# Softmax denominators of four heads in one group of matmuls, reciprocals spread by small transfers

## The reference

```python
xn  = layernorm(x)                       # x: 8 x 512 x 128, float32
qkv = xn @ W_qkv + b_qkv                 # 16 heads of 64
A   = softmax(q @ k.T / 8) per head      # 512 x 512
att = (A @ v) @ W_out + b_out
for t in range(8):                       # a gated recurrence over the 8 batches, from in_c
    c = sigmoid(xn[t] @ wf.T + c @ uf.T + bf) * c + sigmoid(xn[t] @ wi.T + c @ ui.T + bi) * tanh(xn[t] @ wc.T + c @ uc.T + bc)
out = x + att + tanh(xn @ wo.T + c @ uo.T + bo)
```

## Time and profile before

| | |
|---|---|
| median of the runs | 944.82 us |
| the profiled execution | 947.0 us |
| its span, first to last instruction | 945.2 us |
| mean granted TensorE clock | 0.976 of full |
| PEld busy | 570.3 us, 60% |
| DVE busy | 571.0 us, 60% |
| ACT busy | 447.0 us, 47% |

### The profile page before, as it was taken

How to read it: one execution, slowest core, us unless ns; L and a number is a source line. 1 busy time by engine, 2 the same in 40 slices (tenths; PEclk the granted TensorE clock), 3 DMA queues, 4 the chain that set the end, 5 groups by cost and what they waited for, 6 DMA issues and landing times.

```text
span 945.2 us, 14913 instructions
## 1 busy us (share of the span) xinstructions
PE 889.6 (94%) x5429; PEld 570.3 (60%) x5429; DVE 571.0 (60%) x770; ACT 447.0 (47%) x579; POOL 547.4 (58%) x270
## 2 busy tenths in 40 slices
PE   4769899899999999999999999999999999999988
PEld 3445666665666666665666666665666566666553
DVE  6756465564666646664666556665666476664632
ACT  4325545444555534552555554552455455553441
POOL 4033543545777746774677666773677577773664
PEclk9679999999999999999999999999999999999999
DMA  7000000000000000000000000000000000000000
GB/s 223 1 0 1 1 24 1 1 12 2 24 12 2 11 0 34 0 11 0 34 0 11 0 0 34 0 11 0 34 0 11 0 22 11 0 12 1 12 12 11
DMA packets 18635, 13.75 MB, mean 15 GB/s; under 512 B 1298, under 2 KB 16176, under 8 KB 18608
## 3 DMA queue, kind: packets, MB, share of 16 engines
q1 hardware_dynamic: 18608, 13.39, 4.6%
HBM read 6.83 MB, written 2.10 MB: 9 GB/s over the span
## 4 chain that ended last, share of the span: by engine, by line
PE 87%; DVE 9%; ACT 2%; issue 1%; DMA 0%; SPq 0%; DVEq 0%
PE st L744 19%; PE pv L758 13%; PE misc L758 12%; PE mx L725 8%; PE st L690 7%; DVE NM L508 6%; PE mx L774 6%; PE mx L768 6%; PE st L750 5%; PE misc L690 3%; PE misc L647 3%; PE pv L647 2%; PE mx L647 2%; PE pv L690 1%; ACT probs L360 1%; DVE AT L462 1%
## 5 line engine op out<-in xcount | busy, mean ns | idle before, releaser
L508 DVE TENSOR_REDUCE NM<-mx 128x2 f32<-128x1024 f32 x256 | 313.9, 1226 | 174.4 <-PE mx L725 174.2
L360 ACT ACTIVATE probs<-st 128x1024 f32<-128x1024 f32 x256 | 258.3, 1027 | 107.8 <-PE st L750 97.2
L251 POOL TENSOR_TENSOR AT<-AT,RD 128x512 f32<-128x512 f32 x63 | 80.7, 1280 | 256.0 <-DVE RD L526 196.6
L259 POOL TENSOR_TENSOR PSUMK<-probs 128x1024 f32<-128x1024 f32 x64 | 153.1, 2393 | 109.2 <-ACT probs L360 109.2
L265 POOL TENSOR_TENSOR PSUMK<-PSUMK,probs 128x1024 f32<-128x1024 f32 x64 | 152.8, 2387 | 8.2 <-ACT probs L360 2.7
L272 POOL TENSOR_TENSOR PSUMK<-PSUMK,probs 128x1024 f32<-128x1024 f32 x64 | 152.5, 2383 | 6.1
L758 PE MATMUL misc<-probs,VALL 128*64 128x512 f32 x512 | 130.2, 592 | 0.0
L725 PE MATMUL mx<-KH,QH 64*128 64x512 f32 x512 | 114.7, 442 | 13.7 <-DVE NM L508 11.5
L758 PE MATMUL pv<-probs,VALL 128*64 128x512 f32 x512 | 124.7, 606 | 0.0
L744 PE MATMUL st<-QH,KH 64*128 64x512 f32 x512 | 109.0, 420 | 0.8 <-ACT probs L360 0.6
L522 DVE STREAM_TRANSPOSE RD<-mx 128x512 f32<-128x512 f32 x63 | 45.1, 716 | 103.3 <-PE mx L768 103.3
(11 more groups left out here) (179 smaller groups left out, 1237.4 us busy)
## 6 DMA issues: line engine op xcount, KB each, us to landing
probs<-in_L_attn_data_dram SPq DMA_DIRECT2D x4, 512.0 KB, 7.4
XSH<-XH SPq DMA_DIRECT2D x8, 256.0 KB, 2.4
XSL<-XL SPq DMA_DIRECT2D x8, 256.0 KB, 2.4
RES<-in_L_attn_data_dram SPq DMA_DIRECT2D x8, 256.0 KB, 2.7
out_dram<-RES SPq DMA_DIRECT2D x8, 256.0 KB, 2.3
probs<-in_L_attn_W_qkv_dram SPq DMA_DIRECT2D x3, 512.0 KB, 4.5
MROW<-TM SPq DMA_DIRECT2D x64, 4.0 KB
WO<-in_L_attn_W_out_dram SPq DMA_DIRECT2D x1, 512.0 KB, 4.5
```

Of the source, the lines that this page charges most:

```text
L259: nc.gpsimd.tensor_tensor(PSUMK[:, s % 2, :, :], e[:, :, 0, :], e[:, :, 1, :], ALU.add).then_inc(sum_part, 1)
L360: nc.scalar.activation(probs[:, s % 2, :, u, :], st[:, u % 2, :, :], ACT.Exp, scale=SCALE).then_inc(exp_done, 1)
L508: nc.vector.tensor_reduce(NM[:, 0:4 * TB].rearrange("p (h a b) -> p h a b", h=2, a=2)[:, :, s % 2, b], mx[:, :, :], AX.X, ALU.max, negate= ...
```

## The change

- `sums` is called once per stretch, for both pairs, behind all values (in the last stretch ahead of the second pair's values). It has four matmuls of 32 columns, one per head, whose results stand in the four quarters of one bank, `st[:, 1, 1]`. The matmuls of scores that write this bank next wait for DVE (`den_used`).
- DVE makes one transpose and one set of reciprocals per stretch, for four heads (`divisors`). The reciprocals of a head then stand on 32 partitions; eight transfers of SP (`spread_divisors`, 32 partitions by 16 numbers each) put them on the head's 64 partitions in a new tile `RX`, for two pairs. Two transposes fill `RD` from `RX` (`fill_divisors`); they stand between the second and the third reduction of the next stretch, behind a wait for the transfers.
- POOL's two `normalise` move behind the first three sums of the next stretch; the last pair but one is normalised at the very end.

```diff
+            def spread_divisors(n, j):
+
+                sp.wait_ge(r16_done, STRETCHES * n + j + 1)
+                sp.sem_inc(passed_sp, 1)
+                for a in range(2):
+                    for h in range(2):
+                        for m in range(2):
+                            sp.dma_start(RX[HD * h + 32 * m:HD * h + 32 * m + 32, a, :],
+                                         R16[32 * (2 * a + h):32 * (2 * a + h) + 32, :]).then_inc(d_r, 16)
...
                     if j == 3 and not first:
                         sp.wait_ge(out_rows, 16 * n)
                         sp.sem_inc(passed_sp, 1)
+                    spread_divisors(n, j)
...
-                wait(pool, den_done, t - 1)
+                wait(pool, den_done, STRETCHES * n + j)
...
-                    if not (first and j == 0):
-                        normalise(t - 1, s - 1)
                     for k in range(2):
-                        first_sum(t + k, s + k)
+                        first_sum(n, j, t + k, s + k)
                         second_sum(t + k, s + k)
                         third_sum(t + k, s + k)
-                    normalise(t, s)
+                        if k == 0 and not (first and j == 0):
+                            normalise(t - 2, s - 2)
+                            normalise(t - 1, s - 1)
 
             batches(pool, step)
+            normalise(8 * N - 2, PAIRS - 2)
...
-            def divisors(t, s, source):
-
-                r = RD[:, s % 2, :]
-                dve.wait_ge(den_done, t + 1)
-                wait(dve, norm_done, t - 1)
-                nc.vector.transpose(r, source).then_inc(den_used, 1)
-                dve.wait_ge(den_used, t + 1)
-                nc.vector.reciprocal(R16[:, :], r.rearrange("p (c j) -> p c j", j=32)[:, :, 0]).then_inc(r16_done, 1)
-                dve.wait_ge(r16_done, t + 1)
-                nc.vector.transpose(r.rearrange("p (c j) -> p c j", j=32),
-                                    R16[:, :].unsqueeze(2).to_broadcast([P, L // 32, 32])).then_inc(rd_done, 1)
+            def divisors(n, j):
+
+                dve.wait_ge(den_done, STRETCHES * n + j + 1)
+                wait(dve, norm_done, 8 * n + 2 * j)
+                nc.vector.transpose(RD[:, 0, :], st[:, 1, 1, :]).then_inc(den_used, 1)
+                dve.wait_ge(den_used, STRETCHES * n + j + 1)
+                wait(dve, d_r, 128 * (STRETCHES * n + j))
+                nc.vector.reciprocal(R16[:, :], RD[:, 0, :].rearrange("p (c j) -> p c j", j=32)[:, :, 0]).then_inc(r16_done, 1)
+
+            def fill_divisors(n, j):
+
+                dve.wait_ge(d_r, 128 * (STRETCHES * n + j + 1))
+                for a in range(2):
+                    nc.vector.transpose(RD[:, a, :].rearrange("p (c j) -> p c j", j=32),
+                                        RX[:, a, :].unsqueeze(2).to_broadcast([P, L // 32, 32])).then_inc(rd_done, 1)
...
                         maxima(t + 2, s + 2, 0, STRETCHES * n + j + 1)
-                        for b in range(1, TB):
-                            maxima(t + 2, s + 2, b)
+                        maxima(t + 2, s + 2, 1)
+                    if not (first and j == 0):
+                        fill_divisors(n, j - 1)
+                    if coming:
+                        maxima(t + 2, s + 2, 2)
+                        maxima(t + 2, s + 2, 3)
...
-                    divisors(t, s, mx[:, 1, :])
-                    divisors(t + 1, s + 1, mx[:, 0, :] if coming else st[:, 0, 0, :])
+                    divisors(n, j)
 
             batches(dve, step)
+            fill_divisors(N - 1, 3)
...
-            def sums(t, s, dst):
-
-                pe.wait_ge(sum_done, t + 1)
-                for h in range(2):
-                    last = nc.tensor.matmul(dst[OWN[h], :], ones[:, :], PSUMK[:, s % 2, h, :], start=True, stop=True)
+            def sums(t):
+
+                pe.wait_ge(sum_done, t + 2)
+                for a in range(2):
+                    for h in range(2):
+                        g = 32 * (2 * a + h)
+                        last = nc.tensor.matmul(st[g:g + 32, 1, 1, :], ones[:, 0:32], PSUMK[:, a, h, :], start=True,
+                                                stop=True, tile_position=(0, g))
                 last.then_inc(den_done, 1)
...
                         pe.wait_ge(tm_done, STRETCHES * n + j + 1)
-                        wait(pe, den_used, t)
+                        if first:
+                            wait(pe, t_done, 3 * s - 1)
+                        elif j == 1:
+                            pe.wait_ge(o_evac, n)
+                        elif j == 2:
+                            pe.wait_ge(out_done, n)
                         score_maxima(t + 2, s + 2, 0)
                         pe.wait_ge(q_lo, t + 4)
                         pe.wait_ge(k_lo, t + 4)
                     scores(n, t, s, 0)
+                    wait(pe, den_used, STRETCHES * n + j)
                     scores(n, t, s, 1)
...
-                    if first:
-                        pe.wait_ge(t_done, 3 * s + 5)
-                    elif j == 0:
-                        pe.wait_ge(o_evac, n)
-                    elif j == 1:
-                        pe.wait_ge(out_done, n)
-                    sums(t, s, mx[:, 1, :])
...
-                    if coming:
-                        values(n, t + 1, s + 1, (0, 1))
-                        pe.wait_ge(tm_done, STRETCHES * n + j + 2)
-                        sums(t + 1, s + 1, mx[:, 0, :])
-                        values(n, t + 1, s + 1, (2, 3))
-                    else:
-                        sums(t + 1, s + 1, st[:, 0, 0, :])
-                        values(n, t + 1, s + 1)
+                    if not coming:
+                        sums(t)
+                    values(n, t + 1, s + 1)
+                    if coming:
+                        if ahead:
+                            pe.wait_ge(k_lo, t + 6)
+                        sums(t)
```

More of the change, by code:

```diff
@@ L66, in build_block @@
         R16 = sb("R16", [P, L // 32])
+        RX = sb("RX", [P, 2, L // 32])
         RD = sb("RD", [P, 2, L])
@@ L142, in build_block @@
         sum_part, sum_done, norm_done, last_norm = sem("sum_part"), sem("sum_done"), sem("norm_done"), sem("last_norm")
-        d_m = sem("d_m")
+        d_m, d_r = sem("d_m"), sem("d_r")
         d_xs, d_res, out_rows = sem("d_xs"), sem("d_res"), sem("out_rows")
@@ L252, in normalise, with first_sum @@
                                         ALU.mult).then_inc(norm_done, 1)
-            def first_sum(t, s):
+            def first_sum(n, j, t, s):
                 pool.wait_ge(exp_done, 4 * t + 2)
-                wait(pool, den_done, t - 1)
+                wait(pool, den_done, STRETCHES * n + j)
                 e = probs[:, s % 2, :, :, :]
```

## The result

The changed kernel took 1095.3 us (median of 4 runs, 1095.1 to 1098.9) beside 944.9 for the kernel before (4 runs, 944.7 to 945.3): ratio 1.160, 95% interval 1.158 to 1.162. Forecast: 1079, in a range of 1020 to 1110.

What follows compares the result with a forecast made beforehand. TensorE's order was taken to bound every stretch. +4.56 us at 27 starts (+123), +4.2 in the first batch, +2.8 and +4.5 at the end: +135 on 947.0, less 2.2, gives 1079 us; range 1020 to 1110.

Steps and rivals of the forecast that it cites:

- The three parts of the table: Forecast loss by place: 4.2 us up to batch 1, 118.6 over 26 stretches, 11.9 from there to the end.
- What bounds it: Whole kernel: TensorE, busy 94%, sets each stretch's length; a term costs what it adds to its order or waits.
- The sums: Sums on TensorE: one group replaces two, saving 0.86 us per stretch, less 0.25 for the change of shape.
- four tiles do not overlap: Sums on TensorE: the four matmuls run two at a time, so the saving is absent; 1106 us, chance 0.10.
- VectorE at the boundary: VectorE behind the sums: transpose and reciprocal delay the second matmul group of maxima by 0.29 us.
- The transfers: Ahead of the third reduction: eight issues 0.60 us apart delay the filling, and TensorE stands 3.92 us per stretch.
- the rival built on that rule: VectorE's wait before the filling: all transfers land before the second reduction ends; 943 us (938 to 950), chance 0.04.
- The clock: TensorE around the stall: the clock falls to half speed, costing 1.2 us per stretch, bounds 0 and 3.0.
- more at half speed: TensorE behind the stall: low clock costs 1.8 us more at 27 starts; 1127 us, heavier cases together chance 0.11.
- the clock holds: TensorE behind the stall: no fall of clock, 27 x 1.2 us less; 1047 us, chance 0.13 for 1022 to 1047.
- First batch: First batch: sums save 0.61 us four times; three stalls swallow a 2.01 us hole, no clock added; +4.2 us.
- The last stretch: Kernel's end: output projection waits for POOL's later normalisation, +2.8 us, and the final filling comes later, +4.5 us.

Runs made afterwards that it cites:

- the first experiment: Changed kernel with the filling transposes behind the next stretch's reductions, POOL's normalisations one sum group later than planned and the projection in two parts: 947.0 us, ratio 1.001.
- the fifth experiment: the first experiment with the one reciprocal moved behind the first reduction, leaving VectorE only the transpose ahead of it: 938.9 us, ratio 0.9926.
- second experiment: Changed kernel with the filling transposes in place but reading R16 without waiting for the transfers, so divisors go to wrong heads: 950.4 us, ratio 1.0045.
- third: Changed kernel with four of the eight transfers, half of the division left out: 973.8 us, ratio 1.029.
- the fourth experiment: Changed kernel with 22 extra unused matmuls on TensorE in the stall, in every stretch behind the first: 1048.7 us, ratio 1.108.

## Why the prediction was right, and where it was off

The sign, the place and the mechanism came as forecast; the time came 16 us above 1079, inside the range. The three parts of the table miss by 4.4, 4.8 and 4.2 us; the rest is mostly the 2.2 us that the forecast took off for the profiled execution, which this time was no slower than the median. By its own steps:

*What bounds it.* Right: a stretch is TensorE's order, and a stall in front of M3 went into the time in full. With the wait moved out of TensorE's way (the first experiment), no stall in front of M3 is left and 148 of the 150 us are gone.

*The sums.* Right in sign, a little cautious: M0 runs at S+0.99 where I had 1.11. Four matmuls of 32 columns do run side by side, eight records and the change to the next shape in 0.99: the first four start within 0.02 us of each other, the next four 0.45 behind them. The rival "four tiles do not overlap" is out by that row. The Trainium skill's 2.38 times for three such tiles (*TensorE: Matmul & The Clock Gate*, Part 3), by which the group alone would have taken an estimated 1.08, isn't seen here: group and change of shape together took 0.99. How the 0.99 divides between the group and the change behind it was not measured apart; in all the merge is worth 0.68 per stretch, where my terms gave 0.61.

*VectorE at the boundary.* r0 was forecast for S+2.28 and came at 2.53 in the stretch shown (0.40 "issue" in front of it, a batch's start), and earlier in the others. M1 is 0.11 late in three stretches of four and 0.65 in the fourth, where I had 0.29 for all: 0.25 as the mean. That this is the price of the reciprocal in front of r0 is shown by the fifth experiment.

*The transfers.* Right, and by the term that I was least sure of. First issue at S+2.23 (forecast 2.44), distance 0.625 (0.60), all in at S+8.37 (8.44), and r2 at 9.60 (9.87): the two filling transposes take 1.23 to the next instruction and not 1.42. M3 stands 4.01 later than before relative to M0 (9.85 for 5.84), forecast 4.21. Of this 3.3 is the wait and 0.5 to 0.7 VectorE's transposes (second experiment), and each transfer costs 0.635 (third). *DMA: Bandwidth & Descriptors* of the Trainium skill (Issuing engines are not separate DMA queues) has it that initiating a DMA is usually small beside the DMA; here a 2 KB transfer holds SyncE for 0.625 us and lands 1.7 after its issue began, eight take 5.00 us to issue, and the rival built on that rule (938 to 950) is refuted.

*The clock.* The largest miss of a term, and in the direction of the "more at half speed" rival. I had 1.2 us per stretch, with one episode of 3.4 us of which 1.1 would lie in the stall. Three of the 26 stretches had no low clock, and were 3.15 to 3.19 longer than before; 17 had 3.4 us of it, and six had 6.8. From 123.4 in all and 3.17 for the stall and its neighbours, 1.57 is left per stretch: 41 us for the 26, where I had 31 (2.3 of the 41 are the late transfers of three stretches). The two kinds differ in price and in where the fall came:

```profile
291.60:298.40 6.80, 5.84 (x28) 4.62 (x30) 3.29 (x3) 2.05 (x2) 4.87 (x4) 0.50 0.01 2
568.10:571.50 3.40, 3.40 (x18) 2.66 (x16) 1.21 (x1) 1.16 (x2) 2.88 (x3) 0.50 0.00 0
```

In the 17 stretches the fall came between 0.5 us ahead of M3 and 1.5 behind it (M3 is at 567.54 in the second row's stretch), so nearly the whole episode lay on work, and it cost 1.3 to 1.5 us. In the six it came 0.6 to 1.3 ahead of M3 (M3 is at 292.56 in the first row's), the clock stayed down twice as long, and it cost 2.3 to 2.6. I had the fall 1.1 ahead with one episode; that combination occurs in none of the 26. Reading the first batch as "each time" was also too strong: the same four waits of 1.85 us stand in the first experiment, and two of them were followed by a low clock. The stall, on the other side, was a little cheaper than my terms (3.17 for 3.36 without the clock), so that in the sum of the 26 stretches two misses, +10 and -5, partly cancel. The rival "the clock holds" (1047) is close to what the fourth experiment measured once TensorE was kept busy, 1048.7.

*First batch.* The step that was most wrong for its size: +8.6 for +4.2. I let the stall swallow the hole of 2.01 behind M3 and counted no clock, "its clock falls already". The hole did shrink (M3 to the next matmul is 0.73 instead of 2.25, 1.5 us back), but the first twelve of the gate projection's eighteen records behind it ran at half clock, 0.43 apart, as in these rows of the kernel after:

```profile
145.66 0.80 PE L746 MATMUL mx<-KH,QH 64*128 64x512 f32 x2 [3.66 <-DVE NM L521]
146.39 0.80 PE L668 MATMUL pv<-XH,gwH 128*128 128x512 f32 x1
146.98 0.63 PE L668 MATMUL pv<-XH,gwL 128*128 128x512 f32 x1
```

Two of the batch's four stretches had 6.8 us at half clock instead of 3.4. It is 0.8 us in this stretch (6.75 us from the first of its matmuls to the scores behind, for 5.93 before). Another 1.0 is the second stretch, where the eight issues took 5.99 us and M3 came at M0+10.87.

*The last stretch.* +16.1 for +11.9. Both waits came as forecast, and a third thing came with them:

```profile
1063.35 6.93 PE L798 MATMUL mx<-AT,WO 128*128 128x512 f32 x12 [2.52 <-POOL AT L263]
...
1073.79 1.07 PE L791 MATMUL st<-PSUMK,ones 128*32 128x512 f32 x8
...
1084.24 3.78 PE L798 MATMUL mx<-AT,WO 128*128 128x512 f32 x4 [5.80 <-POOL AT L263]
```

The projection waits 2.52 for POOL's normalisation (forecast 2.8), and the last four matmuls start 10.45 behind the sums (forecast 10.65; 6.12 from the sums to their weights before). But each wait brought the clock down: the twelve matmuls took 6.93 us for 5.31, the last four 3.78 for 1.99 before. That is 3.4 of the 4.2 missing.

What stays open: why the fall comes at different places of nearly the same stall, and in three stretches not at all; what held up the issues in the stretches with late transfers; and transfers that are issued by two engines, or fewer and larger ones, which were not tried.

## What to carry to other kernels

Price a merge by its new wait, not by the instructions that it saves: find who stands behind the waiting instruction, in its engine's order, and whether the bounding engine needs it. A small transfer is cheap only where its result is wanted late. With the wait for the same eight transfers between two reductions the kernel lost 150 us, with it behind them under 1 us. Look also at what the late place pushes back: in the first batch it was the recurrence. And when a stall lands on TensorE, add its clock: here half as much again as the stall on average (nothing, 1.4 or 2.4 us beside 3.2), and at the end of the program too.

## What the runs showed of the hardware

- Transfers of 32 partitions by 64 B inside SBUF are issued by SyncE 0.625 us apart (eight in 5.00, four in 2.46) and land 1.7 us after the issue. In five of the 32 stretches of the kernel after, the eight took 5.4 to 6.1 us. The 256 of them moved 0.5 MB and took 164 us of SyncE.
- Four matmul tiles of 128x32, one for each quarter of the array's columns, run at the same time: the first records of the four start within 0.02 us, and eight fp32 records of 512 columns, with the change to 64-row tiles behind them, take 0.99 us. One group of two 64-column tiles (four records) takes 0.86, so the same sums took 1.72 as two groups. Changing from 64-column to 32-column tiles in front of the group adds 0.25 (0.52 from the last record of the values to the sums, for 0.27 with sums of 64 columns).
- Stalls of 3.0 to 3.8 us (4.5 and 4.8 in two) brought the granted clock from full to 0.50 in 23 of 26 stretches, for 3.4 or 6.8 us. Behind the first batch of the kernel with four transfers, 25 stalls of 0.5 to 1.2 us and one of 2.1 were followed by no fall; with matmuls in the stall, late transfers left 1.8 and 2.0 us of it in two stretches, and both were followed by one. Matmuls without use, issued into the stall, kept the clock at full in the others and gave back some 47 us.
